# Three rotating homes of 120 rows: x loaded in place, bias tiles in both stages, every load and store begun on SyncE

## What is computed

```python
rel = tril(idx[:, None] - idx[None, :])
nd = log(abs(c * rel) + 1) / (log(abs(c * pos) + 1) + EPS)
bias = einsum('qkm,mh->qkh', relu(nd[..., None] * W1[0] + b1), W2) + b2
x = x + bias.transpose(2, 0, 1)[None]
...
ret = einsum('BGMTS,GMN->BGNTS', x, w + eye)
ret += einsum('BGITS,BTGIM->BGMTS', einsum('BGMTS,BTGIM->BGITS', x, qw1), qw2)
ret += einsum('BGMTS,BTGM->BGMTS', x, qdd)
# the same two once more with kw1, kw2, kdd, which depend on s instead of t
```

## Time and profile before

| | before |
|---|---|
| median of 3 runs | 1029.08 us (1028.45 to 1029.82) |
| the profiled execution | 1017.06 us, of which the span from first to last instruction is 1015.1 us |
| PE matmul, busy | 755.0 us (74%) |
| ACT, busy | 453.8 us (45%) |
| DVE, busy | 373.5 us (37%) |
| POOL, busy | 344.3 us (34%) |
| moved by DMA | 149.50 MB |

### The profile page before, as it was taken

One profiled execution on the slowest core, in us unless ns is written; L12 is line 12 of the kernel. 1 busy time (PEld: TensorE's weight loads), 2 busy tenths in 40 slices (PEclk: granted clock), 3 DMA queues, 4 the chain that ended last, 5 costly groups with the idle time before them and its releaser, 6 DMA issues.

```text
span 1015.1 us, 37021 instructions
## 1 busy us (share of the span) xinstructions
PE 755.0 (74%) x17186; PEld 545.3 (54%) x17186; DVE 373.5 (37%) x358; ACT 453.8 (45%) x472; POOL 344.3 (34%) x189
## 2 busy tenths in 40 slices
PE   2269697688767796697965978777796687867973
PEld 1029654486536753485534955347553485534963
DVE  7970265205640274204541045310354103541041
ACT  6554264444553263443653435534264443653400
POOL 7461044202440053202863027630276402771000
PEclk9679988798979997789999989979899798996997
DMA  6974799844997178943899138892388923790079
GB/s 112 204 163 82 191 201 238 191 103 107 226 205 175 41 164 214 200 107 85 179 203 201 47 85 183 206 191 49 83 154 211 200 67 79 168 214 3 5 161 194
DMA packets 366437, 149.50 MB, mean 147 GB/s; under 512 B 99660, under 2 KB 366028, under 8 KB 366284
## 3 DMA queue, kind: packets, MB, share of 16 engines
q1 hardware_dynamic: 229068, 80.02, 39.3%
q10 hardware_dynamic: 137216, 67.13, 27.6%
HBM read 77.61 MB, written 69.47 MB: 145 GB/s over the span
## 4 chain that ended last, share of the span: by engine, by line
PE 42%; SPq 15%; ACTq 15%; ACT 9%; issue 8%; DMA 4%; POOL 3%; DVE 3%; POOLq 0%; DVEq 0%
PE main L609 22%; ACTq L196 15%; PE main L599 11%; PE bias L622 9%; SPq L223 9%; ACT hidden L376 4%; SPq L230 4%; POOL hidden L339 3%; ACT hidden L371 3%; DMA mats_a<-a_mats 3%; ACT y L385 2%; DVE mixed L510 1%; DMA a_mats<-mixed 1%; DMA b_mats<-mixed 1%; DVE y L523 1%
## 5 line engine op out<-in xcount | busy, mean ns | idle before, releaser
L339 POOL TENSOR_TENSOR hidden<-log_table,row_scale 128x1024 f32<-128x1024 f32 x176 | 340.1, 1950 | 573.4 <-PE bias L622 560.7
L376 ACT ACTIVATE hidden<-hidden,b_col 128x1024 f32<-128x1024 f32 x176 | 197.6, 1144 | 293.6 <-issue 153.5
L622 PE MATMUL bias<-hidden,w_blocks 128*64 128x512 f32 x768 | 229.9, 714 | 129.2 <-ACT hidden L376 84.3
L510 DVE TENSOR_TENSOR mixed<-main,mixed 128x1024 f32<-128x1024 f32 x128 | 156.7, 1224 | 440.0 <-PE main L599 440.0
L599 PEld LDWEIGHTS main<-y,mats_a 32*32 32x32 f32 x8192 | 241.9, 131 | 121.2 <-issue 58.4
L599 PE MATMUL main<-y,mats_a 32*32 32x128 f32 x8192 | 271.3, 280 | 42.1 <-DMA mats_a<-a_mats 28.0
L609 PE MATMUL main<-y,mats_b 32*32 32x128 f32 x8192 | 258.0, 281 | 51.1 <-issue 37.8
L609 PEld LDWEIGHTS main<-y,mats_b 32*32 32x32 f32 x8192 | 243.3, 132 | 74.4 <-issue 46.5
L398 ACT ACTIVATE mixed<-main 128x1024 f32<-128x1024 f32 x128 | 130.9, 1023 | 199.5 <-PE main L609 194.2
L622 PEld LDWEIGHTS bias<-hidden,w_blocks 128*64 128x64 f32 x768 | 54.8, 155 | 233.5 <-issue 189.3
L523 DVE SCALAR_TENSOR_TENSOR y<-bias,b_col,x_stage 128x1024 f32<-128x1024 f32 x64 | 82.2, 1284 | 142.7 <-PE bias L622 142.7
(11 more groups left out here) (37 smaller groups left out, 27.5 us busy)
## 6 DMA issues: line engine op xcount, KB each, us to landing
x_stage<-in_x SPq DMA_DIRECT2D x512, 128.0 KB, 5.3
out_mixed<-mixed ACTq DMA_DIRECT2D x256, 128.0 KB, 4.4
out_mixed<-mixed ACTq DMA_DIRECT2D x128, 256.0 KB
mats_a<-a_mats SPq DMA_DIRECT2D x256, 32.0 KB
b_mats<-mixed SPq DMA_DIRECT2D x2, 512.0 KB, 6.1
mats_b<-b_mats SPq DMA_DIRECT2D x8, 128.0 KB, 2.8
a_mats<-mixed SPq DMA_DIRECT2D x2, 512.0 KB, 9.5
mixed<-in_L_conv_kw SPq DMA_DIRECT2D x2, 128.0 KB, 2.6
```

The costliest lines, as they stand in the source:

```text
L339: nc.gpsimd.tensor_tensor(hidden_tile(h).rearrange("p (j s) -> p j s", j=ROWS), bass.AP(logs.tensor, logs.offset, [list(logs.ap[0]), [1, R ...
L376: nc.scalar.activation(hidden_tile(h), hidden_tile(h), ACT.Relu, bias=b1_col[:, 0:1])\
L510: dve.tensor_tensor(at, main[:, T % 2, :].rearrange("p (t s) -> p t s", t=ROWS), at, ALU.add).then_inc(main_taken, 1)
L622: mm = pe.matmul(bias[into, T % 2, at:at + BANK], w2_blocks[:, g, :], hidden_tile(hidden_index(k, T, g))[:, at:at + BANK], start=True, sto ...
```

## The change

There are nine regions instead of eight: the first of 8 tiles (64 rows), then eight of 15 tiles (120 rows). A b tile's matmuls stream 64 or 120 columns instead of 128, and there are 9 x 16 b tiles instead of 128; the a tiles and bias tiles remain 128 each.

`y`, `x_stage` and `mixed` become one buffer, `homes`: three homes of 15 tiles. Region k has its y in home k mod 3 and its sums in home (k + 2) mod 3. x is loaded one tile slot behind its y place, and `add_bias` (now two instructions a tile, by parity of the row) writes y in front of it. The x of region k + 2 is loaded into the home whose sums have been stored, so a load waits for stores (`out_done`), no longer for `y_ready`. The first b tile of a region no longer waits for stores.

The bias tiles of region k + 1 are spread over both stages of region k, at step `bias_step` (1, 3, ... 29 of 31 for two regions of 15 tiles). `take_b` alternates between ScalarE and VectorE after region 0. The hidden ring has 3 tiles. The row-by-row form is gone. The scales of the second half are loaded in two parts.

Every store moves from ScalarE to SyncE (`PORTIONS = (0,)` leaves none), and both loads and stores go in larger pieces: of 1 to 4 tiles, with 8 DMAs a piece, 64 KB a tile in each DMA. `mats_a` is loaded with 2 DMAs a chunk instead of 8, each of 128 KB, still in pieces of 128 bytes. The small constants are loaded from ScalarE's queue. In SyncE's order, a region's stores, the loads of the next matrices and of x stand behind one another, in the order of the a tiles. In the set-up, only 8 tiles of y are made ahead of the first b tile; the a matrices are turned at step 4 of region 0.

```diff
+COL_TILES = W // ROWS
...
+REGION_TILES = (8,) + (15,) * 8
+REGIONS = len(REGION_TILES)
+FIRST_TILE = [sum(REGION_TILES[:k]) for k in range(REGIONS)]
+ALL_TILES = S // ROWS
+HALF_TILES = ALL_TILES // 2
+HOME_TILES = max(REGION_TILES)
+HOMES = 3
+STORE_PIECES = {8: (2, 3, 3), 15: (2, 3, 3, 3, 4)}
+LOAD_PIECES = {8: (1, 3, 4), 15: (1, 3, 3, 3, 4, 1)}
+PORTIONS = (0,)
 CHUNK = 32
...
+CHUNK_TILES = CHUNK // ROWS
+CHUNKS = S // CHUNK
+A_RING = 2
+A_SIZE = GS * H * CHUNK
+RING = 3
 SETUP_TILES = 4
+TURN_AT = 4
...
-        mixed = sb("mixed", [P, W, W])
+        homes = sb("homes", [P, HOMES * HOME_TILES * COLS])
...
+        def bias_step(k, T):
+            return 1 + T * (COL_TILES + REGION_TILES[k] - 3) // (REGION_TILES[k + 1] - 1)
+        def bias_tile_at(k, s):
+            if k + 1 < REGIONS:
+                for T in range(REGION_TILES[k + 1]):
+                    if bias_step(k, T) == s:
+                        return T
+            return None
...
+        def y_slot(k, T):
+            return k % HOMES * HOME_TILES + T
+        def x_slot(k, T):
+            return (y_slot(k, T) + 1) % (HOMES * HOME_TILES)
+        def mixed_slot(k, T):
+            return (k + 2) % HOMES * HOME_TILES + T
...
+        def y_rows(into, k, T, b):
+            at = homes[into, y_slot(k, T) * COLS:y_slot(k, T) * COLS + COLS]
+            return at.rearrange("p (j s b) -> p b j s", s=W, b=2)[:, b]
...
+            def load_x(k, i):
+                T, n = piece_start(load_pieces(k), i), load_pieces(k)[i]
+                if k >= 1 and T + 1 >= HOME_TILES:
+                    sp.wait_ge(out_done[0], times(STORE_PIECES, 0, k - 1) * PER_PIECE)
+                elif k >= 2 and T + 1 < REGION_TILES[k - 2]:
+                    left = piece_of(store_pieces(k - 2), min(T + n, REGION_TILES[k - 2] - 1))
+                    sp.wait_ge(out_done[left], times(STORE_PIECES, left, k - 2) * PER_PIECE)
+                t0 = tile_of(k, T) * ROWS
...
                 for b in range(BLOCKS):
...
+                    sp.dma_start(home_rows(b, x_slot(k, T), n * ROWS),
+                                 x[0, :, t0:t0 + n * ROWS, b * W:(b + 1) * W]).then_inc(x_in[i], DMA)
...
+            def load_mats_a(v):
+                if v >= A_RING:
+                    sp.wait_ge(main_ready, a_tile_of((v - A_RING + 1) * CHUNK_TILES - 1) + 1)
+                slot = v % A_RING
+                for b2 in range(GS):
+                    into = bass.AP(mats_a, (b2 * A_RING + slot) * A_SIZE + b2 * CHUNK,
+                                   [[GS * A_RING * A_SIZE, GROUPS * H], [GS * CHUNK, H], [1, CHUNK]])
+                    sp.dma_start(into, bass.AP(a_mats.tensor, v * H * H * CHUNK,
+                                               [[0, GROUPS], [H * CHUNK, H], [1, H * CHUNK]]))\
+                        .then_inc(a_in[slot], DMA)
...
             load_compact("b", kw1, kw2, kdd)
-            load_x(0)
-            load_x(1)
+            load_x(0, 0)
             load_compact("a", qw1, qw2, qdd)
             sp.dma_start(w_eye, w.rearrange("g m n -> g (m n)").partition_broadcast(P)).then_inc(weights_in["a"], DMA)
-            for q in range(2, XSLOTS):
-                load_x(q)
+            load_x(0, 1)
+            load_x(0, 2)
             save_mats("b")
             sp.wait_ge(mats_out["b"], 2 * DMA)
...
+            sp.wait_ge(mats_zeroed, 2)
             load_mats_b()
...
-                load_x(q)
+            for i in range(3):
+                load_x(1, i)
             save_mats("a")
+            load_x(1, 3)
+            sp.wait_ge(mats_out["a"], 2 * DMA)
+            for v in range(A_RING):
+                load_mats_a(v)
+            load_x(1, 4)
             sp.wait_ge(tables_made, 3)
             sp.dma_start(late_scales, scale_late).then_inc(scales_out, DMA)
...
+                while k + 1 < REGIONS and loaded[k + 1] < 5:
+                    load_x(k + 1, loaded[k + 1])
+                    loaded[k + 1] += 1
+                if k == 2:
+                    sp.wait_ge(scales_out, DMA)
+                    sp.wait_ge(nd_ready, PART // 2 // ROWS)
+                    sp.dma_start(row_scale[:, 0:PART // 2], late_scales[:, 0:PART // 2]).then_inc(scales_in, DMA)
+                if k == 4:
+                    sp.wait_ge(nd_ready, PART // ROWS)
+                    sp.dma_start(row_scale[:, PART // 2:], late_scales[:, PART // 2:]).then_inc(scales_in, DMA)
+                for T in range(REGION_TILES[k]):
+                    for i in range(len(store_pieces(k))):
+                        if T == piece_start(store_pieces(k), i + 1) - 1:
+                            taken, count = emptied(a_tile(k, T))
+                            sp.wait_ge(taken, count)
+                            for b in range(8):
+                                store_block(sp, k, i, b).then_inc(out_done[i], DMA)
+                    v, last = divmod(tile_of(k, T), CHUNK_TILES)
+                    if last == CHUNK_TILES - 1 and v + A_RING < CHUNKS:
+                        load_mats_a(v + A_RING)
+                    if k + 1 < REGIONS and T == min(6, REGION_TILES[k] - 4):
+                        load_x(k + 1, 5)
+                    if k + 2 < REGIONS and T in (7, 10, 13):
+                        load_x(k + 2, loaded[k + 2])
+                        loaded[k + 2] += 1
+            for i in range(5):
+                sp.wait_ge(out_done[i], times(STORE_PIECES, i, REGIONS - 1) * PER_PIECE)
...
+            for u in range(ALL_TILES):
...
+                if t0 == PART + PART // 2:
+                    pool.wait_ge(scales_in, 2 * DMA)
+                for g in range(groups_of(u)):
+                    h = hidden_index(u, g)
+                    if h >= RING:
+                        pool.wait_ge(hidden_used, h - RING + 1)
...
+            act.dma_start(c_col[:], c.partition_broadcast(P)).then_inc(consts_in, DMA)
...
+            def make_hidden(u):
+                for g in range(groups_of(u)):
+                    act.wait_ge(nd_ready, hidden_index(u, g) + 1)
+                    nc.scalar.activation(hidden_tile(u, g), hidden_tile(u, g), ACT.Relu, bias=b1_col[:, 0:1])\
+                        .then_inc(hidden_ready, 1)
...
+                if tile_of(k, T):
+                    act.wait_ge(y_const_ready, tile_of(k, T))
+                for b in range(2):
+                    add = nc.scalar.activation(y_rows(high_half, k, T, b), x_rows(high_half, k, T, b),
+                                               ACT.Identity, bias=b2_col[high_half, 1:2])
+                add.then_inc(y_const_ready, 1)
...
+                nc.scalar.activation(mixed_columns(k, C), column_sums(k, C), ACT.Copy)\
+                    .then_inc(main_taken[b_tile(k, C) % 2], 1)
...
+            for T in range(REGION_TILES[0]):
+                make_hidden(tile_of(0, T))
...
+                add_const_bias(0, T)
+                if T == 2:
+                    take_turned("b")
             for k in range(REGIONS):
...
+                if k + 1 < REGIONS:
+                    make_hidden(tile_of(k + 1, 0))
+                for s in steps(k):
...
+                    if s == TURN_AT and k == 0:
+                        take_turned("a")
+                    if s < COL_TILES and (k == 0 or s % 2 == 0):
+                        take_b(k, s)
+                    T = bias_tile_at(k, s)
+                    if T is not None:
+                        if T + 1 < REGION_TILES[k + 1]:
+                            make_hidden(tile_of(k + 1, T + 1))
+                        add_const_bias(k + 1, T)
...
+            def take_b(k, C):
...
+                dve.wait_ge(main_ready, b_tile(k, C) + 1)
+                dve.tensor_copy(mixed_columns(k, C), column_sums(k, C)).then_inc(main_taken[b_tile(k, C) % 2], 1)
...
+                    dve.wait_ge(y_ready, u)
+                if u == HALF_TILES:
+                    dve.wait_ge(y_const_ready, HALF_TILES)
...
+                for b in range(2):
+                    add = dve.scalar_tensor_tensor(
+                        out=y_rows(rows, k, T, b), in0=falling(u, b, 0 if both else b * (P // 2), P if both else P // 2),
+                        scalar=b2_col[rows, 0:1], in1=x_rows(rows, k, T, b), op0=ALU.add, op1=ALU.add)
+                add.then_inc(y_ready, 1)
+            for T in range(REGION_TILES[0]):
                 add_bias(0, T)
-                if T == 1:
-                    take_turned("b")
...
+            compact("a")
+            dve.wait_ge(logs_made, 4)
...
-                for T, U in phase_steps():
+                for s in steps(k):
+                    if s >= COL_TILES:
+                        finish_tile(k, s - COL_TILES)
+                    elif k and not (s % 2 == 0):
+                        take_b(k, s)
+                    T = bias_tile_at(k, s)
...
-                        add_bias(k + 1, U)
+                        add_bias(k + 1, T)
+                    if k == 0 and T == 1:
+                        invert(row_scale[:, W:])
```

(31 more changed lines are left out.)

## The result

The changed kernel takes 1075.12 us (median of 4 runs, 1073.99 to 1081.85); the kernel before, run beside it, 1029.45 us. The ratio is 1.0501, 95% interval 1.044 to 1.0561: 5% slower. The forecast was 854 us, within 780 to 930, and faster. The profiled execution has a span of 1073.3 us and came out at 1075.1, 1.8 us more; the forecast had put 1.18% on top of that, which has no counterpart here.

What follows compares the result with a forecast made beforehand. Instruction fetch, delayed by other DMAs, was to bound the regions: 106 + 3 x 88 + 4 x 90.4 + 68 + 28 (late matrices) + 14 = 842 us of span, 844 x 1.0118 = 854 us measured, range 780 to 930.

Steps and rivals of the forecast that it cites:

- The step that failed: SyncE's single queue: a region's 16.7 MB at 214 GB/s take 78 us, below the 88 of instruction fetch.
- slower than before: Rival, chance 0.04: loads and stores in one ring hold each other up; at 135 GB/s a region takes 124 us, 1068 in all.
- `mats_a` late: SyncE's order in the a stage: one matrix load late in most regions, 4 us in each of seven, 28 in all.
- x late for bias tiles: Sign that the forecast is wrong: bias tiles of the b stage wait for x; the forecast had x in time.
- the last rival: Late x sends b-stage bias tiles back to the a stage: up to 96 us, 951 measured; counted within a 0.2 chance.
- waits of x for stores (`out_done`) are covered: SyncE's x loads: their waits for stores cost nothing, as the last pieces are wanted over 20 us later.
- Hidden tiles: TensorE's 84.3 us of waits for ScalarE's hidden tiles go; up to 0.5 us per bias tile kept in the range.
- Fetch: Instruction fetch, delayed by other DMAs, takes 5.5 us per 128 pairs: 88 us in regions 1 to 3, 90.4 in 4 to 7.
- Work of TensorE: Matmul times: an a tile 1.80 us, a b tile of 120 columns 1.70, a bias tile 1.19 or 2.05 more.
- The clock mostly full: Sign to look for: TensorE's granted clock mostly full, against 0.6 to 0.9 in most slices before.
- Start and end: First b tile at 46 us, first a tile at 84, region 0 ends at 106; region 8 takes 68, the end 14.

Runs made afterwards that it cites:

- m1: Bare copy of x to the output through SBUF, nothing computed, all loads and stores on SyncE's queue: 693.31 us.
- e3: The changed kernel with `mats_a` loaded for the first two chunks only, 30 of 32 loads left out (wrong output): 949.34 us, ratio 0.9361 to the kernel before.
- e5: The changed kernel with `mats_a` issued ahead of the store of the same tile, still on SyncE: 1044.76 us, ratio 1.032 to the kernel before.
- c1: The changed kernel with stores and `mats_a` both on ScalarE, x alone on SyncE: 1127.28 us, ratio 1.1122 to the kernel before.
- e1: The changed kernel with all stores on ScalarE again in small portions, loads still on SyncE: 991.28 us, ratio 0.9773 to the kernel before.
- e2: The changed kernel with only the `mats_a` loads moved to ScalarE, stores and x still on SyncE: 962.81 us, ratio 0.9467 to the kernel before.
- m2: The bare copy m1 with its stores on ScalarE's queue instead of SyncE's: 534.57 us.
- m3: The bare copy m1 with 32 chunk loads in the form of `mats_a` (128-byte pieces) added on SyncE's queue: 948.86 us.
- m5: The bare copy m3 with the chunk loads, still on SyncE, landing in runs of 2 KB: 778.51 us.
- m4: The bare copy m3 with the 128-byte-piece chunk loads on ScalarE's queue instead: 753.55 us.
- c2: The changed kernel with `mats_a` and half of each store's blocks on ScalarE, the other half and x on SyncE: 1057.09 us, ratio 1.0422 to the kernel before.

## Why the prediction was wrong

**The step that failed** is "the bytes are 7.86 MB in, 7.86 MB out and 1.0 of matrices, 16.7 MB, at 214 GB/s 78 us. Below 88, so it is not the bound". It has two errors. The 214 GB/s of rows 5 were measured with two queues at work, stores on ScalarE's. That error alone is small: at m1's 194 GB/s a region takes 86 us, still below 88. The other is that the matrices were priced by bytes. By the copies a region's share of one ring, with chunk loads, is 16.7 MB / 151 GB/s = 111 us. Regions 1 to 7 in fact took 829 us, 118 each, or 141 GB/s, and the forecast had 654 with the late matrices. That 175 us is three quarters of the miss in the span (1073 - 842 = 231).

**The rival that came true** is "slower than before", with a chance of 0.04: one ring that carries loads and stores in order, deciding from 118 us a region, 141 GB/s. Its mechanism and its point were there; that its price of 1068 us is so near to the 1075 measured is in part luck, as it had 124 us a region and nothing of the 41 us that region 0 took more than forecast. What makes the loads hold each other up, the short pieces of `mats_a`, it did not name. The argument against it was that 180 to 214 were reached "wherever work was queued". The 214 was a rate of two queues, and the 180 one of x loads alone, without matrices or stores between them.

**`mats_a` late.** I took one late load a region, 4 us each, 28 in all, with 0 and 70 as bounds. There were 16 waits, 111.5 us on PE. The order on SyncE was read rightly, and the delays in it were sized with issues of 0.6 us, where the load itself holds the ring. As a cause of time, the loads are 117 us (e3), and their place 19 of it (e5). (The 62 us of issue that I gave for a region come to 60 by its own medians; nothing rests on it.)

**x late for bias tiles** was named in the last rival and as a sign to look for. It came: 110.6 us of VectorE's waits, 65.4 on TensorE. That "waits of x for stores (`out_done`) are covered" was right as written, for SyncE never waited there. What failed is the reason given, that the last pieces of x "are wanted in the second half of the b stage, over 20 us later": x comes late because it stands in the queue behind stores, their waits and the chunk loads.

**Hidden tiles.** Right: 84.3 us of waits to 7.8, with a ring of 3. No gain of it is seen in the time, as the stages waited elsewhere; c1, where these waits come back, shows that they can cost.

**Fetch.** 60 to 90 us of gaps within tiles were forecast; those of PE L686 and L675 put to "issue" are 63.1 and 9.4 us, 72 together. (The kernel before had 51.6 of them.) That they are fetch was argued from counts, and the trace bears it out: 41 of the 43 such gaps end 1.2 to 1.7 us after a packet of 16 KB of the instruction queue has ended, and such a packet comes only every 7.5 us. That other DMAs delay it was not tested. The price was right; what bound a region was another term, 111 to 118 us of ring against 88 of fetch.

**Work of TensorE.** a tiles 1.80 us, right (e3's clean stages). For a b tile of 120 columns I took 1.70 between 1.64 and 1.75; the lower bound is right (timeline of TensorE in region 8):

```profile
979.65 3.50 PE L686 MATMUL main<-homes,mats_b 32*32 32x120 f32 x128 [0.26 <-issue]
```

Two tiles take 3.50 us where rows 6 have 3.77, in proportion to the columns (120/128). That is 0.06 us on each of 128 tiles, some 8 us over the run, in the other direction.

**The granted clock** was not in the sum. "The clock mostly full" was too hopeful: it stands at 0.50 for 281 us of the trace (223 before), and TensorE works in 138 us of that, so up to 69 us of its work are owed to 1.2 GHz. The kernel before had 152 us of work there, so the change did not make this worse; the sum left it out, because its rows were read at full clock. The clock falls mostly in and right behind the waits: the row 255 to 260 has 0.50, and in the rows below 64 pairs take 3.64 us behind a gap of 13 us and 2.05 before it. In e3, where the waits for matrices are gone, 90 us of work lie there, 45 at most, and whole a stages run at 1.00. So a wait of TensorE costs more than its length; e1 to e3 hold this cost in their ratios.

**Start and end.** First b tile 48.0 us (forecast 46), first a tile 96.2 (84), region 0 ends at 146.8 (106), region 8 takes 81 us up to its last addition instead of 68, and from there 16.4 us are left instead of 14. (The 11.6 us of the kernel before run from the start of its last addition, not from its end, and so do these.) Region 0 has the largest miss of these, 41 us:

```profile
102.39 2.05 PE L675 MATMUL main<-homes,mats_a 32*32 32x128 f32 x64
117.48 3.64 PE L675 MATMUL main<-homes,mats_a 32*32 32x128 f32 x64 [13.03 <-DVE homes L581]
...
146.80 3.43 PE L686 MATMUL main<-homes,mats_b 32*32 32x120 f32 x64 [14.01 <-DVE homes L599]
```

(TensorE's timeline in that a stage.) Two gaps make 27 us, and both are x late. VectorE waited 13.99 us for it before the first, and before the second:

```profile
145.23 1.51 DVE L599 SCALAR_TENSOR_TENSOR homes<-bias,b_col,homes 64x512 f32<-64x512 f32 x2 [14.13 <-DMA homes<-in_x]
```

SyncE begins the piece for the first at 94.4 us, behind the first two chunks of matrices, the last piece of region 1 at 136.6, behind two stores and a chunk load. I had let x come in time there.

**What remains open.** e2 and e3 come to 0.9467 and 0.9361, some 974 and 963 us on the scale of 1029, against 854 forecast. The low clock (45 to 55 us at most), the late x (57 and 79 us of TensorE's waits, summed as above) and the start are together of that size, but they overlap, and how they share it was not separated. It is not the rate of the queue: e2's 139 MB at m1's 194 GB/s are 718 us. The place is known in e3: there the a stages of regions 1 to 7 take 301 us in all, which is what the forecast's 5.5 us for 128 pairs give (302), and the b stages 411 us where the same gives 323. Nor was x put past the stores.

## What to carry to other kernels

A rate read from a trace belongs to the queues that were at work in it: before every load and store goes to one queue, ask for the rate of that queue alone, and get it from a bare copy. Price a DMA by the time that it holds up what stands behind it, not by its bytes; issue times well above their minimum are the sign of it, and a long second issue of two alike points at the form of that DMA itself. In this kernel it paid most to move the small-piece loads, not the bulk, to a second queue, and to put no more there than its engine can issue without standing still in its own arithmetic.

## What the runs showed of the hardware

- One queue with both directions moves 194 GB/s on average, two with one direction each 252 (m1, m2, once each).
- A 262 KB load (2 DMAs) in pieces of 128 bytes adds 8.0 us to a copy in whose queue it stands, in runs of 2 KB 2.7 us, and from another queue 1.9 us (m3, m5, m4). The second of its two DMAs takes 6.0 us to issue in m3 and 7.2 in an otherwise empty queue (m4).
- A DMA issue of 0.5 to 0.6 us at least takes up to 5.7 us on SyncE in the changed kernel (L295, chunk loads), and on ScalarE up to 10.6 for a store and 14.2 for a chunk load in c2. In c1 ScalarE issues for 594 us and computes during 126 of them.
- Instruction blocks of 16 KB: 41 of 43 gaps within tiles end 1.2 to 1.7 us after such a packet has ended (the changed kernel).
- Matmuls of 120 columns take 3.50 us for two tiles (128 pairs) against 3.77 with 128 columns: no step, but about in proportion.
